# The first stage of a four-layer network on one core: batch norm and qkv products on image pairs instead of single images

## The reference, cut to what matters

```python
mean = jnp.mean(x, axis=(0, 2, 3), keepdims=True)
var = jnp.var(x, axis=(0, 2, 3), keepdims=True)
xn = (x - mean) * jax.lax.rsqrt(var + EPS)
xn = xn * bn_gamma[None, :, None, None] + bn_beta[None, :, None, None]
qkv = _conv1x1(xn, qkv_w, qkv_b).reshape(Bx, 3, HEADS, HD, Hx, Wx)   # 192 -> 576 channels
q, k, v = (qkv[:, 0], qkv[:, 1], qkv[:, 2])
scale = HD ** (-0.5)                                                 # q is scaled by it
```

## Time and profile before

| | us |
|---|---|
| median of 3 runs | 6283.86 (6279.79 to 6284.36) |
| the profiled execution's own time | 6284.17 |
| its span | 6282.3 |
| first matmul of the products (L295) | 60.70 |
| last eviction of the products (L253) | 324.29 |
| first load of the next stage | 332.06 |

### The profile page before, as it was taken

One profiled execution on the slowest core, in us unless ns is written; L12 is line 12 of the kernel. 1 busy time (PEld: TensorE's weight loads), 2 busy tenths in 40 slices (PEclk: granted clock), 3 DMA queues, 4 the chain that ended last, 5 costly groups with the idle time before them and its releaser, 6 DMA issues. The chain is left out here.

```text
span 6282.3 us, 86905 instructions
## 1 busy us (share of the span) xinstructions
PE 5356.1 (85%) x34576; PEld 2449.1 (39%) x34576; DVE 4338.2 (69%) x5109; ACT 2745.5 (44%) x3903; POOL 837.4 (13%) x898
## 2 busy tenths in 40 slices
PE   6959999999978995988869799968958888888877
PEld 2434544545543442445544333323313333333323
DVE  3267777777741112238978388884879999999978
ACT  1213333333331221225541354434658767867833
POOL 0000000000000001112235000001123333323300
PEclk9989999999989997999989999988979999999989
DMA  6431212112103113434443100102320000000035
GB/s 152 124 61 34 39 20 39 34 25 40 20 10 97 68 43 114 133 119 136 141 141 127 54 18 27 35 18 85 104 70 6 26 26 14 27 26 6 15 104 153
DMA packets 305695, 397.63 MB, mean 63 GB/s; under 512 B 160300, under 2 KB 282740, under 8 KB 302044
## 3 DMA queue, kind: packets, MB, share of 16 engines
q1 hardware_dynamic: 282268, 290.07, 17.2%
q0 software_dynamic: 23040, 102.18, 4.7%
HBM read 225.68 MB, written 166.50 MB: 62 GB/s over the span
## 5 line engine op out<-in xcount | busy, mean ns | idle before, releaser
L3631 DVE TENSOR_TENSOR_SCAN s_h<-s_da,s_h 128x448 f32<-128x448 f32 x672 | 745.3, 1171 | 1.5 <-ACT s_da L3558 1.4
L3478 PE MATMUL s_py<-s_prod,s_idf 128*128 128x448 f32 x1344 | 584.2, 557 | 24.4 <-ACT s_ycol L3571 23.2
L504 PE MATMUL b_pc<-b_ca,b_wdm 128*113 128x392 f32 x1152 | 487.4, 520 | 56.9 <-DVE b_idb L877 55.5
L3558 ACT ACTIVATE s_da<-s_dt,s_al 128x448 f32<-128x448 f32 x672 | 405.7, 656 | 199.3 <-DVE s_h L3631 148.9
L636 ACT ACTIVATE b_band<-b_psel 124x784 f32<-124x784 f32 x192 | 158.3, 824 | 604.8 <-PE b_psel L561 604.7
L504 PE MATMUL b_pc<-b_cb,b_wdm 128*113 128x392 f32 x960 | 409.2, 526 | 0.0
L3616 DVE TENSOR_TENSOR s_h<-s_dtu,s_pb 128x896 f32<-128x896 f32 x336 | 370.6, 1103 | 29.2 <-POOL s_dtu L3665 23.1
L3638 DVE TENSOR_TENSOR s_prod<-s_h,s_pc 128x896 f32<-128x896 f32 x336 | 376.4, 1120 | 0.1
L929 DVE TENSOR_SCALAR b_band<-b_psel 124x784 f32<-124x784 f32 x192 | 186.9, 973 | 265.5 <-PE b_psel L561 263.4
L2678 DVE SCALAR_TENSOR_TENSOR j_zc<-j_zt,j_gw,j_zc 128x896 f32<-128x896 f32 x336 | 360.3, 1147 | 0.0
L3478 PEld LDWEIGHTS s_py<-s_prod,s_idf 128*128 128x128 f32 x1344 | 248.5, 192 | 219.3 <-issue 166.7
(11 more groups left out here) (624 smaller groups left out, 11318.9 us busy)
## 6 DMA issues: line engine op xcount, KB each, us to landing
mid_qkvp<-a_out SPq DMA_DIRECT2D x84, 372.0 KB, 4.0
b_qk<-mid_qkvp SPq DMA_DIRECT2D x96, 240.2 KB
d_vt<-mid_vd SPq DMA_DIRECT2D x200, 96.0 KB
d_qs<-mid_qd SPq DMA_DIRECT2D x20, 744.0 KB, 5.5
d_ks<-mid_kd SPq DMA_DIRECT2D x20, 744.0 KB, 7.8
b_v<-mid_qkvp SPq DMA_DIRECT2D x6, 1922.0 KB
mid_pout<-d_out POOLq DMA_DIRECT2D x20, 558.0 KB, 4.3
mid_x1p<-c_out POOLq DMA_DIRECT2D x14, 744.0 KB, 4.0
```

Source lines behind the costliest of these rows:

```text
L504: mm = pe.matmul(pc[n % 2][0:113, 0:392], wdm[:, slot, p, 0:113], src, start=(w == STARTS[a]), stop=(w + 1 == STARTS[a + 1]))
L3478: mm = pe.matmul(y, idf[:, :], prod[j % 3][:, e, :], start=(pr == 0 and e == 0), stop=False)
L3558: last = a.activation(da[j % 4][:, e, :], dt[s % 2][:, span(c)], ACT.Exp, scale=al[:, u, n:n + 1])
L3631: v.tensor_tensor_scan(x, along(da[j % 4][:, e, :]), x, before_, ALU.mult, ALU.add).then_inc(scanned, 1)
```

## The change

`batchnorm_qkv` is rewritten to work on image pairs.

- x lies in SBUF as 2 pairs x 3 tiles of 128 partitions and is loaded with six DMAs of 1568 KB on SP's queue. The weights are given twice (2 x 192 rows) and are loaded, with gamma, beta and the bias, on POOL's queue. BATCH_NORM_STATS run on each tile as it lands, 42 in all, and there are three aggregates.
- A channel's two halves of the statistics now lie on two partitions, 64 apart. A matmul with a permuted identity (`a_swap`, loaded on ACT's queue) brings each its other half, four copies line them up, and seven small operations merge mean and variance.
- The bias products are twelve matmuls again: full ones and ones of 64 rows.
- The products run over 14 steps (pair, chunk), unrolled. A step makes nine output tiles of 128 partitions: tiles 2j and 2j + 1 hold output channels 128j to 128j + 127 of image 0 and image 1 for j = 0 to 3, and the ninth the last 64 channels of both. There are twenty matmuls, eight PSUM banks, three output buffers. Products also wait for the first addition of the bias.
- POOL sets zeros, waits for all of x, and stores the borders. In each step SP stores image 0 and POOL image 1, six DMAs each (three of 128 partitions, three of 64); both wait for all nine evictions.

```diff
-        xs = sb("a_x", [G, 2, B, N])
-        out = [sb(f"a_out{i}", [G, 6, 8, PW]) for i in range(2)]
-        ps = [ctx.enter_context(nc.psum_tensor(f"a_ps{i}", [G, 512], F32)) for i in range(4)]
+        xs = sb("a_x", [128, PAIRS, 3, N])
+        out = [sb(f"a_out{i}", [128, 9, 8, PW]) for i in range(OB)]
+        ps = [pt(f"a_ps{i}") for i in range(8)]
...
+        def store(eng, s, i, stored):
+            q, c = divmod(s, NCH)
+            b = 2 * q + i
+            o = out[s % OB]
...
+            eng.wait_ge(even_out, evens(9 * (s + 1)))
+            eng.wait_ge(odd_out, odds(9 * (s + 1)))
+            for t, c0, n, j, p in ((0, 0, 128, i, slice(0, 128)), (0, 128, 64, 2 + i, lo), (1, 0, 64, 2 + i, hi),
+                                   (1, 64, 128, 4 + i, slice(0, 128)), (2, 0, 128, 6 + i, slice(0, 128)), (2, 128, 64, 8, half)):
+                eng.dma_start(img(t, c0, n), tile(j, p)).then_inc(stored[s % OB], 16)
...
         @block.sync
-            for b in range(B):
-                sp.dma_start(xs[:, :, b, :], xv[b]).then_inc(x_loaded[b], 16)
-            sp.dma_start(wt[:, :, :], qkv_wT.rearrange("(g p) o -> p g o", g=2)).then_inc(par_loaded, 16)
+            for q in range(PAIRS):
+                for t in range(3):
+                    sp.dma_start(xs[:, q, t, :], xv[q, :, t, :]).then_inc(x_loaded[3 * q + t], 16)
+            for s in range(STEPS):
+                store(sp, s, 0, first_stored)
...
+        @block.gpsimd
+            p.dma_start(wt[:, :, :], qkv_wT.rearrange("(t p) o -> p t o", p=128)).then_inc(par_loaded, 16)
...
+            for i in range(3 * PAIRS):
+                p.wait_ge(x_loaded[i], 16)
+            p.wait_ge(zero_set, 1)
+            for t in range(3):
+                for r in (0, PW - 3):
...
+                    p.dma_start(dst, zero[:, :, :]).then_inc(border_stored, 16)
+            for s in range(STEPS):
+                store(p, s, 1, second_stored)
...
         @block.vector
+            v.wait_ge(swapped, 1)
+            got = ps[0][:, 0:6].rearrange("p (t k) -> p t k", k=2)
+            v.tensor_copy(other[lo, 0:2, :], got[lo, 1:3, :]).then_inc(taken, 1)
...
+            v.tensor_tensor(half[:, :], mv[:, :, 0], other[:, :, 0], ALU.add).then_inc(merged, 1)
+            v.tensor_tensor(gap[:, :], mv[:, :, 0], other[:, :, 0], ALU.subtract).then_inc(merged, 1)
+            v.tensor_tensor(var[:, :], mv[:, :, 1], other[:, :, 1], ALU.add).then_inc(merged, 1)
...
         @block.tensor
+            pe.matmul(ps[0][:, 0:6], swap[:, :], mv[:, :, :].rearrange("p t k -> p (t k)"), start=True, stop=True).then_inc(swapped, 1)
...
+            pe.wait_ge(folded, 6)
+            pe.wait_ge(bias_step, 1)
...
-                        for g in range(2):
-                            last = pe.matmul(ps[n % 4][:, 0:CH], wf[:, g, m * G:(m + 1) * G],
-                                             xs[:, g, b, c * CH:(c + 1) * CH], start=(g == 0), stop=(g == 1))
-                        last.then_inc(product, 1)
+            for s in range(STEPS):
+                q, c = divmod(s, NCH)
+                x0, x1, x2 = (xs[:, q, t, c * CH:(c + 1) * CH] for t in range(3))
+                for j in range(4):
+                    n = 9 * s + 2 * j
+                    col = slice(128 * j, 128 * j + 128)
+                    first = free(n)
+                    pe.matmul(first[:, 0:CH], wf[:, 0, col], x0, start=True, stop=False)
+                    second = free(n + 1)
+                    pe.matmul(first[:, 0:CH], wf[lo, 1, col], x1[lo, :], start=False, stop=True).then_inc(product, 1)
+                    pe.matmul(second[:, 0:CH], wf[hi, 1, col], x1[hi, :], start=True, stop=False)
+                    pe.matmul(second[:, 0:CH], wf[:, 2, col], x2, start=False, stop=True).then_inc(product, 1)
+                n = 9 * s + 8
+                both = free(n)
+                pe.matmul(both[lo, 0:CH], wf[:, 0, 512:576], x0, start=True, stop=False)
+                pe.matmul(both[hi, 0:CH], wf[:, 2, 512:576], x2, start=True, stop=False)
+                pe.matmul(both[lo, 0:CH], wf[lo, 1, 512:576], x1[lo, :], start=False, stop=True)
+                pe.matmul(both[hi, 0:CH], wf[hi, 1, 512:576], x1[hi, :], start=False, stop=True).then_inc(product, 1)
```

More of the change, by code:

```diff
@@ new lines, in _ @@
+                    p.dma_start(dst, zero[:, :, :]).then_inc(border_stored, 16)
+            for s in range(STEPS):
+                store(p, s, 1, second_stored)
+            for o in range(OB):
+                p.wait_ge(second_stored[o], 16 * 6 * len(range(o, STEPS, OB)))
+            p.wait_ge(border_stored, 16 * 6)
+        @block.scalar
+        def _(a):
+            a.dma_start(swap[:, lo], ident[:, hi]).then_inc(swap_loaded, 16)
+            a.dma_start(swap[:, hi], ident[:, lo]).then_inc(swap_loaded, 16)
+            a.wait_ge(merged, 9)
+            a.activation(std[:, :], var[:, :], ACT.Sqrt, bias=EPS).then_inc(std_done, 1)
+            a.wait_ge(bias_step, 3)
+            a.wait_ge(zero_set, 1 + OB)
+            for s in range(STEPS):
+                if s >= OB:
+                    a.wait_ge(first_stored[s % OB], 16 * 6 * (s // OB))
+                    a.wait_ge(second_stored[s % OB], 16 * 6 * (s // OB))
+                for j in range(9):
+                    n = 9 * s + j
+                    if n % 2 == 0:
+                        a.wait_ge(product, n + 1)
+                        a.activation(out[s % OB][:, j, :, 3:3 + W], ps[n % 8][:, 0:CH].rearrange("p (h w) -> p h w", w=W),
+                                     ACT.Identity, bias=bias[:, j // 2:j // 2 + 1]).then_inc(even_out, 1)
@@ L217, in _ @@
         @block.vector
         def _(v):
[L219 to L221 removed]
+            for q in range(PAIRS):
+                for t in range(3):
+                    v.wait_ge(x_loaded[3 * q + t], 16)
                     for c in range(NCH):
[L223 removed]
+                        last = v.bn_stats(stats[:, t, q * NCH + c, :], xs[:, q, t, c * CH:(c + 1) * CH])
@@ L257, in _ @@
[L257 to L272 removed]
+            for t in range(3):
+                v.bn_aggr(mv[:, t, :], stats[:, t, :, :]).then_inc(merged, 1)
@@ new lines, in _ @@
+            v.tensor_tensor(bias[:, :], ps[1][:, 0:5], qb[:, :], ALU.add).then_inc(bias_step, 1)
+            v.wait_ge(bias_step, 1)
+            v.tensor_scalar(bias[:, 0:1], bias[:, 0:1], HD ** -0.5, None, ALU.mult).then_inc(bias_step, 1)
+            v.tensor_scalar(bias[lo, 1:2], bias[lo, 1:2], HD ** -0.5, None, ALU.mult).then_inc(bias_step, 1)
+            v.wait_ge(bias_step, 3)
+            v.wait_ge(zero_set, 1 + OB)
+            for s in range(STEPS):
+                if s >= OB:
+                    v.wait_ge(first_stored[s % OB], 16 * 6 * (s // OB))
+                    v.wait_ge(second_stored[s % OB], 16 * 6 * (s // OB))
+                for j in range(9):
+                    n = 9 * s + j
+                    if n % 2:
+                        v.wait_ge(product, n + 1)
+                        v.tensor_scalar(out[s % OB][:, j, :, 3:3 + W], ps[n % 8][:, 0:CH].rearrange("p (h w) -> p h w", w=W),
+                                        bias[:, j // 2:j // 2 + 1], None, ALU.add).then_inc(odd_out, 1)
@@ L274, in _ @@
         @block.tensor
         def _(pe):
[L277 to L297 removed]
+            pe.wait_ge(swap_loaded, 32)
```

204 lines of the change are left out of this document (99 added, 105 removed).

## The result

The changed kernel takes 6197.82 us (median of four executions, 6190.26 to 6214.94), the kernel before on the same chip 6284.11: a ratio of 0.9868, with a 95% interval of 0.9845 to 0.989, so 86 us less and clear of no change. The time lies 7.8 us above the 6190 of the prediction and inside its range.

A forecast was written before the change was run, and what follows sets the result against it. Stage one was taken as bound by the load, then by TensorE's issue in the products. Products -83.0, chain -12.9 and tail +1.6 sum to -94.3 us, taking 6284.2 to 6190 us; range 6181 to 6211.

The forecast's parts named there:

- Load: Loading x in stage one: 128-partition transfers at 404 GB/s, last tile at 31.1 us, statistics ending at 34.8.
- the load still ends last: Stage-one load: VectorE's statistics need only 22.4 us in all, so the load, not VectorE, sets the end.
- Chain to the first product: From last statistics through aggregates, swap, small operations and bias products: first product at 47.8 instead of 60.7, -12.9 us.
- Products: Product piece of stage one: fourteen steps of 12.65 us plus slow start, 180.5 us instead of 263.5, -83.0 us.
- both serial rivals: Products: pair halves run one after the other, 63 us more (chance 0.04); same-bank corners likewise, 10.5 us more (0.04).
- the slow start: Start of the product piece: matmuls first run at slower spacing, costing 3.45 us, kept from the old kernel.
- the waits at the old boundaries and their sequel: Old product piece: 5.0 us of TensorE waits at three image boundaries plus 2.5 of slow spacing, both expected to go.
- stores give some of it back: Rival, chance 0.08: stores fill the three output buffers in some steps, TensorE waits 3 to 10 times, costing 12 to 40 us.
- Stores within the products: Product steps: 168 stores on SP and POOL, 181 GB/s on average, hidden except the last step's.
- The tail: Stage one's end, from last product to next stage's first load: 9.4 us instead of 7.8, +1.6 us.
- POOL's queue becomes the bound: Rival, chance 0.02: POOL's six stores a step set the pace; at 4 us each, 159 us more, 6349 us.

The follow-up runs named there:

- two kernels with cut transfers: Changed kernel with each x tile loaded in two transfers, of 96 and 32 partitions or of 64 and 64: 6220.51 and 6221.04 us.
- the kernel that has the halves apart: Changed kernel with the second image's half-depth matmul issued after its full one, so no two halves are neighbours: 6263.43 us.
- the kernel with ScalarE's queue: Changed kernel with the second image's stores issued from ScalarE's queue instead of POOL's: 6186.68 us, ratio 0.9854.

## Why the prediction was right, step by step

**Load: right.** The rate was taken from the 128-partition rows at 404 GB/s; the windows show 345 to 432. Statistics end at 34.12, forecast 34.8. One step of it was not so: "the load still ends last". VectorE has no gap from the fourth tile on, so the end is set by its own 21 statistics from 22.82 on, and a faster load of the last tiles alone would not have ended them sooner. The two kernels with cut transfers show that the partitions of a transfer make the rate, as argued.

**Chain to the first product: right in kind, 2.3 us too long.** Aggregates 1.50 (1.5), swap 0.60 (1.0), small operations 2.91 (4.0), bias products and addition 5.70 (6.5). The small operations came out shorter because many do not depend on each other: three vectors of one step start 0.08 us apart, while the 0.25 that I took from the old chain is the distance of dependent ones. I had taken the last four bias products at the price of the first eight; being 64 columns wide, they are 0.30 apart, not 0.51. The chain is 10.7 us long in place of 13.0, within its bounds of 9 to 16; together with the statistics, 0.7 earlier, this makes the term -15.9 in place of -12.9.

**Products: right.** A step is 12.62 us, forecast 12.65, put together from blocks of two other stages. Pairs and corners run together, and both serial rivals are refuted; in the kernel that has the halves apart the lost pairing costs 61 us, made up otherwise than the rival's 63. The one term mis-sized is the slow start, kept at 3.45 from an execution in which it was long: half of 4.0 us in the changed kernel, 2.0, and 1.6 in the kernel with ScalarE's queue. The 7.5 us that I gave to the waits at the old boundaries and their sequel measured 7.4 when they were taken away alone (8.8 less the luck of the start). But the rival "stores give some of it back" put the 2.5 of slow spacing on every wait, where the sum has it once for three waits and the trace of before shows it after one of them: at a third of it each, 3 to 10 waits would be 7 to 25 us and not 12 to 40.

**Stores within the products: right.** 182 and 180 GB/s in the windows from 100 to 200 us against 181 worked out; no buffer is waited for. GpSimd issues a store in 0.55 us, below the 0.75 that I took.

**The tail: the step that failed.** "From the last product to the next stage that makes 0.9 + 4.5 + 3.5 + 0.5 = 9.4 in place of 7.8: +1.6." It measured +12.0. Two things were missed. The larger is the drain of GpSimd's queue at the barrier: 7.90 us with 96 DMAs on it, on the path because GpSimd's own stores are the last ones. With those stores on another queue, the end takes 10.8 to 12.1; with half of them on SP's queue and none of GpSimd's in the last step, 11.5. I could have read its price before, but I looked at the issue and the landing of a store alone. The trace of before has such drains at other barriers:

```profile
L1003 POOLq DRAIN  x1: 1540/1540/1540, 2372.2 to 2372.2; - x1
```

This one stands behind 18 DMAs of GpSimd, of 744 KB for the most part. Behind 6, 20 and 28 there it is 0.54, 1.69 and 2.35 us, all within 0.02 of the line through 12, 54 and 96, and behind 67 and 83 it is 5.59 and 7.58, 0.05 and 0.75 above it. So it goes by the number of DMAs, not by their bytes. The smaller is the landing: the last stores were complete 10.8 us after the start of the last eviction (234.2 - 223.4) where the forecast had 8.9; the issues began 1.2 us after it and took 3.2, in place of 0.9 and 4.5, but the last one landed 6.3 after that and not 3.5. The barrier's steps around the drain took 1.1 where it had 0.5. That is the other 2.5. The forecast let this term move by 2 us; it moved by 10.4. The rivals "stores give some of it back" and "POOL's queue becomes the bound" sought the price of that queue within the steps, where it is nothing; it stood after them.

**The sum.** The two terms that were too cautious nearly hid the one that was wrong: -88.9 measured for the stage, -94.3 forecast. The profiled execution then came to within 0.4 us of the forecast only because the untouched stages happened to take 4.8 us less in it. That closeness is luck; the median is 7.8 above.

## What to carry to other kernels

Put a transfer on all 128 partitions before tuning anything else about it, and when contraction rows are left over, order them so that two halves on opposite sides of the array stand next to each other. When stores move to GpSimd's queue, add the drain at the next barrier to the sum, some 0.08 us for each DMA up to about a hundred, unless the queue's last work ends that much before the others'. And check each term against its own two events in the trace: here the total was right within its range while one of three terms was off by more than ten microseconds.

## What the runs showed of the hardware that I had not expected

- GpSimd's drain grows by 0.0815 us a DMA from 12 to 96 DMAs in the stage, takes 10.35 us at 138 and only 4.96 at 180. Why it falls is open. A long drain need not come from DMAs: in the trace of before two with no DMA on the queue take 6.39 and 9.20 us (at 0.9 and 3509.9), as long as memsets of GpSimd still run there.
- Transfers of 96 + 32 and of 64 + 64 partitions both load x at 195 to 257 GB/s with the DMA engines at a share near 1, where those of 128 partitions load it at 345 to 432.
- Twelve matmuls of one column, 3.2 to 3.3 us of a TensorE that counts as busy, were followed by a granted clock of 0.50 to 0.60 where full products or idle matmuls had just before brought it to the quick spacing (two kernels); behind 17.6 us of idle matmuls without a gap they were not.
- A window's granted clock says nothing ahead of the trace's first clock record: it prints 1.00 from 44 to 48 us in the changed kernel and up to 77 in the one with the halves apart, where the spacing is the double one.
- The slow stretch at the start is not of fixed length: 3.2 to 6.2 us where pairs and full matmuls alternate (eight kernels), 33 us where single halves and full ones do (one execution), TensorE being busy in both. What decides this and the point on the bias products was not tried further.
